# A state-space layer and a mixture of experts on one core: every engine's order, the stage lags and the PSUM banks laid out anew, and the combine weights broadcast over 128 rows instead of 40

## What is computed

```python
x = x + S6(layernorm(x))      # state-space layer, HIDDEN = 256, 16 states, rank 64, 4 taps
x = x + MoE(layernorm(x))     # 8 experts of width 176, top 2, and a shared MLP of width 352

# S6:  u, o = split(x @ W_in.T);  u = silu(conv4(u) + conv_b)
#      delta_lo, b, c = split(u @ W_gate.T);  delta = softplus(delta_lo @ W_delta.T + bias)
#      h_t = exp(A * delta_t) * h_(t-1) + (delta_t * u_t) * b_t      for 256 x 16 states
#      y_t = sum_s h_t * c_t + D * u;   out = (y * sigmoid(o) * o) @ W_out.T
# MoE: scores = softmax(x @ gate_w.T); top-2 weights, normalised, times 2.5 -> combine
#      sum_e combine[e] * (silu(x @ w_gate[e]) * (x @ w_up[e])) @ w_down[e]  + shared MLP
```

## Time and profile before

| | before |
|---|---|
| time, three runs | 1216.91, 1220.03, 1220.68 us; median 1220.03 |
| profiled execution | span 1213.8 us from the first to the last instruction; no time of its own is given beside the span |
| busy over the span | PE 1121.7 us (92%), DVE 1069.3 (88%), POOL 1068.8 (88%), ACT 1003.7 (83%), PEld 918.1 (76%) |
| TensorE clock granted | 0.972 of 2.4 GHz on average |
| DMA engines | 37.0% of their time |

### The profile page before, as it was taken

How to read it: one execution, slowest core, us unless ns; L and a number is a source line. 1 busy time by engine, 2 the same in 40 slices (tenths; PEclk the granted TensorE clock), 3 DMA queues, 4 the chain that set the end, 5 groups by cost and what they waited for, 6 DMA issues and landing times. The chain is left out here.

```text
span 1213.8 us, 25690 instructions
## 1 busy us (share of the span) xinstructions
PE 1121.7 (92%) x9075; PEld 918.1 (76%) x9075; DVE 1069.3 (88%) x1702; ACT 1003.7 (83%) x2115; POOL 1068.8 (88%) x502
## 2 busy tenths in 40 slices
PE   5667999999999999999999999999999999998887
PEld 4445887787878778788887877778777778876676
DVE  5568999999998999999999999999999999998854
ACT  5878888988887898888889888888888888887642
POOL 3899999999998999999999999999999999998820
PEclk8768999999999999999999999999999999998899
DMA  7433444343334434324443433344343334433000
GB/s 195 121 96 81 111 110 110 85 115 85 83 104 108 106 89 115 87 79 107 112 111 80 115 93 78 103 111 111 80 115 102 80 92 110 107 94 91 5 6 9
DMA packets 71481, 115.05 MB, mean 95 GB/s; under 512 B 8173, under 2 KB 30394, under 8 KB 71354
## 3 DMA queue, kind: packets, MB, share of 16 engines
q1 hardware_dynamic: 71354, 113.42, 37.0%
HBM read 41.04 MB, written 5.24 MB: 38 GB/s over the span
## 5 line engine op out<-in xcount | busy, mean ns | idle before, releaser
L423 POOL TENSOR_TENSOR inject<-rep,bc 128x1024 f32<-128x1024 f32 x256 | 605.7, 2392 | 26.3 <-DMA rep<-dd 26.3
L433 POOL TENSOR_TENSOR read<-state,bc 128x1024 f32<-128x1024 f32 x192 | 453.4, 2384 | 11.7 <-DVE state L702 10.2
L702 DVE TENSOR_TENSOR_SCAN state<-decay_ps,inject 128x1024 f32<-128x1024 f32 x192 | 431.6, 2276 | 20.1 <-ACT decay_ps L526 19.3
L526 ACT ACTIVATE decay_ps<-rep,neg_a 128x255 f32<-128x255 f32 x1024 | 425.4, 461 | 8.2 <-DVE state L702 3.4
L1004 PE MATMUL acc_ps<-ffn_down,features 128*128 128x128 f32 (+1 forms) x1792 | 244.8, 281 | 0.5 <-DVE features L731 0.5
L1004 PEld LDWEIGHTS acc_ps<-ffn_down,features 128*128 128x128 f32 (+1 forms) x1792 | 220.3, 192 | 23.2 <-issue 6.6
L970 PE MATMUL work_ps<-xn2T_part,ffn_gate 128*128 128x256 f32 x1344 | 218.4, 299 | 5.8 <-ACT g_silu L513 3.0
L513 ACT ACTIVATE g_silu<-work_ps 128x512 f32<-128x512 f32 x224 | 134.6, 601 | 104.5 <-PE work_ps L970 93.3
L970 PEld LDWEIGHTS work_ps<-xn2T_part,ffn_gate 128*128 128x128 f32 x1344 | 179.4, 192 | 51.3 <-ACT g_silu L513 21.8
L979 PE MATMUL work_ps<-xn2T_part,ffn_up 128*128 128x256 f32 x1344 | 192.5, 283 | 0.0
L723 DVE TENSOR_TENSOR features<-g_silu,work_ps 128x512 f32<-128x512 f32 x224 | 150.0, 681 | 46.0 <-PE work_ps L979 45.4
(11 more groups left out here) (134 smaller groups left out, 1244.5 us busy)
## 6 DMA issues: line engine op xcount, KB each, us to landing
rep<-dd SPq DMA_DIRECT2D x256, 256.0 KB, 4.7
bc<-bc_rows SPq DMA_DIRECT2D x64, 512.0 KB, 4.8
x_in<-in_L_attn_x_dram SPq DMA_DIRECT2D x32, 128.0 KB, 2.1
out_dram<-result SPq DMA_DIRECT2D x32, 128.0 KB, 1.8
bc_rows<-g_sb SPq DMA_DIRECT2D x32, 32.0 KB
state<-in_L_ffn_w_gate_dram SPq DMA_DIRECT2D x1, 704.0 KB, 4.5
inject<-in_L_ffn_w_up_dram SPq DMA_DIRECT2D x1, 704.0 KB, 6.0
ffn_down<-in_L_ffn_w_down_dram SPq DMA_DIRECT2D x1, 704.0 KB, 7.2
```

The costliest lines, as they stand in the source:

```text
L423: pool.tensor_tensor(inject[:, at % RI], du_all, b_all, ALU.mult).then_inc(inject_done, 1)
L433: pool.tensor_tensor(read[:, at % RR], state[:, at % RS], c_all, ALU.mult).then_inc(read_done, 1)
L526: last = act.activation(decay_ps[:, at % 2, j, 1:T], rep[(HALVES * n + half) % RP][:, j, 0, 1:T], ACT.Exp, scale=neg_a[:, col:col + 1])
L702: dve.tensor_tensor_scan(to, decays, inject[:, at % RI].rearrange("p j t -> p (j t)"), 0.0, ALU.mult, ALU.add).then_inc(state_done, 1)
```

## The change

2. The banks change, and so do the explicit waits that guard them:

```diff
-GATE_BANK = [0, 2, 1, 0, 0, 0, 0]
-UP_BANK = [1, 0, 2, 1, 1, 2, 1]
+GATE_BANK = [2, 0, 0, 1, 0, 1, 2]
+UP_BANK = [1, 2, 0, 1, 0, 0, 2]
-COMB_BANK = [0, 1, 0, 1, 0, 1]
+COMB_BANK = [1, 1, 0, 2, 0, 2]
-        combT_ps = banks[1][0:LOW + EXPERTS, 0:T]
+        combT_ps = banks[2][:, 0:T]
-        xnT_ps = banks[2][:, 0:T]        # xn2T_ps and logit_ps likewise go from 2 to 1,
+        xnT_ps = banks[1][:, 0:T]        # marked_ps, inv_ps and comb_ps from 1 to 2
```

3. The combine weights are padded with zeros to 128 rows:

```diff
-        csel = sb("csel", [LOW + EXPERTS, ROUTED], F32R)
+        csel = sb("csel", [P, ROUTED], F32R)
-        comb_parts = sb("comb_parts", [P, TILES, LOW + EXPERTS], F32R)
-        combT = sb("combT", [LOW + EXPERTS, T], F32R)
+        comb_parts = sb("comb_parts", [P, TILES, P], F32R)
+        combT = sb("combT", [P, T], F32R)
```

4. Two of the new order's explicit waits, on PE and on ACT:

```diff
+                if on(2):
+                    pe.wait_ge(u_done, k + 3)
+                if on(-2):
+                    gates(k - 2, 6)
...
+                if on(-2):
+                    act.wait_ge(h_done, PAIRS * (k - 2) + 4)
...
+                if later(1):
+                    softplus(k + 1)
+                    copy_delta(k + 1)
```

More of the change, by code:

```diff
@@ new lines, in copy_z, with softplus, copy_delta @@
+            def copy_z(n):
+                act.wait_ge(delta_done, n)
+                act.wait_ge(z_mm, n + 1)
+                act.copy(z_sb[:], z_ps).then_inc(z_copied, 1)
+            def softplus(n):
+                act.wait_ge(z_copied, n)
+                act.activation(delta_ps, z_sb[:], ACT.Softplus).then_inc(delta_done, 1)
+            def copy_delta(n):
+                act.wait_ge(delta_done, n + 1)
+                for half in range(HALVES):
+                    act.wait_ge(rep_in[half], 16 * JB * n)
+                act.copy(dd[:, :, 0, :], delta_ps).then_inc(dd_done, 1)
@@ L646, in body @@
+                if later(2):
+                    copy_g(k + 2)
                 if on(0):
@@ L671, in body @@
-                if on(1) and k >= 0:
-                    decays(k + 1, 0)
-                    decays(k + 1, 1)
-            step(body, -3)
-            steps(body, -2)
+                if later(2):
+                    copy_z(k + 2)
+                if later(1):
+                    decays(k + 1, 0)
+            log_vars(-4)
+            rstds(-4)
+            act.preload_act_table_set("silu_and_others")
+            norm1(0)
+            xn_high(0)
+            xn_low(0)
+            copy_weights()
@@ new lines, in body @@
+                if on(-2) and not on(1):
+                    dve.wait_ge(h_done, PAIRS * (k - 2) + 2)
+                if on(-2):
+                    route(k - 2)
+                    gated_up(k - 2, 2)
+                    comb_low(k - 2)
+                if on(-3):
+                    add_result(k - 3)
+                if on(0):
+                    scan(k, 2)
+                if on(-1):
+                    add_x1(k - 1)
+                    stats_x1(k - 1)
+                if later(3):
+                    moments_x(k + 3)
@@ new lines, in project_g, with project_z @@
+            def project_g(n):
+                if n == 0:
+                    pe.wait_ge(act_weights, ACT_WEIGHTS)
+                pe.wait_ge(u_done, n + 1)
+                for half in range(HALVES):
+                    last = pe.matmul(g_ps, wg[:, half, :], u[n % RU][:, half, :], start=(half == 0),
+                                     stop=(half == HALVES - 1))
+                last.then_inc(g_mm, 1)
+            def project_z(n):
+                pe.wait_ge(g_done, n + 1)
+                for half in range(HALVES):
+                    last = pe.matmul(z_ps[:, half, :], wdelta[:, half, :], g_sb[:], start=True, stop=True)
+                last.then_inc(z_mm, 1)
@@ new lines, in skip_term, with sum_states @@
+            def skip_term(n, half):
+                pe.matmul(y_ps, skip[:, half, :], u[n % RU][:, half, :], start=True, stop=False, skip_group_check=True)
+            def sum_states(n, q):
+                half, g = divmod(q, SG)
+                if q in OWN:
+                    pe.wait_ge(read_own_done, own(n, q) + 1)
+                    products = read_own
+                else:
+                    pe.wait_ge(read_done, others(n, q) + 1)
+                    products = read[:, others(n, q) % RR]
+                for j in range(JB):
+                    last = pe.matmul(y_ps[j * CB:(j + 1) * CB, :], sum_sel[:], products[:, j, :],
+                                     start=False, stop=(g == SG - 1), skip_group_check=True)
+                last.then_inc(sum_done, 1)
@@ new lines, in down @@
+            def down(n, chunk, fresh=False):
+                r = rows(chunk)
+                if chunk in (0, 2):
+                    pe.wait_ge(h_done, PAIRS * n + chunk // 2 + 1)
+                elif chunk == NSH or chunk % 2 == 0:
+                    pe.wait_ge(hc_done, COMBS * n + (chunk - NSH + 1) // 2 + 1)
+                for j in range(TILES):
+                    last = pe.matmul(down_ps[:, j * DIM:(j + 1) * DIM], features[0:r, chunk, j * P:(j + 1) * P],
+                                     ffn_down[0:r, chunk, :], start=fresh and j == 0, stop=(chunk == CHUNKS - 1),
+                                     skip_group_check=True)
+                last.then_inc(down_mm, 1)
@@ L1032, in body @@
[L1032 to L1036 removed]
+                    gate_rows(k + 1)
+                if on(-1):
+                    pe.wait_ge(y_taken, HALVES * (k - 1) + 2)
+                if on(-3):
+                    down(k - 3, 10)
@@ L1194, in body @@
[L1194 to L1204 removed]
+                    down(k - 2, 4)
```

1298 lines of the change are left out of this document (644 added, 654 removed).

## The result

| | before | after |
|---|---|---|
| time, median of the runs beside each other | 1218.47 us (1215.77 to 1220.68) | 1170.2 us (1168.76 to 1170.26) |
| span of the profiled execution | 1213.8 | 1168.5 |

The ratio is 0.9598, 95% interval 0.9572 to 0.9623. The forecast was 1200.4 us; the gain is more than twice what it said, and the time lies under the range.

A forecast was written before the change was run, and what follows sets the result against it. A loop of waits through POOL, PE and ACT was taken to bound the kernel at 35.0 us; 30 periods x (35.02 - 34.3) = 21.6 saved, 2 lost at the end, span 1194.2, plus 6.2: 1200.4 us, range 1180 to 1232.

The forecast's parts named there:

- ACT's work: ACT's busy time a step: 30.58 us before plus 2.57 for two table loads and 0.2 for gaps, 33.4.
- ends: Before the first and after the last x1: start unchanged, tail 2 us longer from two table loads.
- The loop of before: Sum 6, gates(0), silus, softplus, delta copy, rep spreads, I0, R5, R6: 35.0 us, the old period; 32.0 after the change.
- Wait (a), silu 6: ACT at silu 6 waits 0.45 us for gates(6), which wait for `u`, with only silu 5 between.
- Wait (b), copy_g: ACT at copy_g waits 0.35 to 0.4 us for project_g: PE needs 6.05 us, ACT 5.75.
- (c), xn2_low: PE's rest product done at t + 9.15, ACT there at t + 9.2 (t: end of `u`): no wait, no slack.
- 128 rows: PE's 11 spreads a step, padded from 40 rows, each save 0.06 us, 0.65 in all; without padding period 34.9.
- DVE, POOL, banks, DMA: DVE's pass 33.7 us, POOL's 33.1 plus about 1 of waits, moved b/c spreads hidden, new guards 0.
- the wait for rstd: POOL's wait for ACT's rstd, 66.1 us in all before, would be gone, that for rep kept.
- the third: Rival in which ACT runs without waits: period 33.5 us, 43 us faster, 1177 us; chance 0.12.

The follow-up runs named there:

- x1_before_sum6: Kernel before with PE's sum 6 moved behind ups(2) of the next step, beside sum 7; 1225.04 us, ratio 1.0044.
- y1_after_rows40: Kernel after with the combine weights back at 40 rows in place of 128; 1206.88 us, ratio 0.9889 to the kernel before.
- y4: Kernel after with an eighth table load a step, ahead of copy_z; 1222.89 us, ratio 1.0033 to the kernel before.
- v2b: Kernel after with norm 1 whole between silus 5 and 6 and downs 3 and 4 behind xn2's rest product; 1177.74 us.
- v2c: Kernel after with norm 1 in halves, one between silus 5 and 6, and downs 3 and 4 behind xn2's rest product; 1178.27 us.
- v2a: Kernel after with only downs 3 and 4 moved behind xn2's rest product on PE; 1175.74 us.

## Why the prediction was wrong

The direction was right, and so was the kind of sum for the new period, ACT's work and two waits of it; its terms were off. What failed are two of them: ACT's work, put at 33.4 us and measured at 33.05, and the wait at copy_g, put at 0.35 to 0.4 and measured at 0.10. The reading of the old period was in part wrong as well. Span saved: 19.6 us by the forecast, 45.3 measured. The 25.7 us of difference are

- **the period**, 34.3 against 33.77, and 31 of them in place of 30: 31 x 1.25 - 30 x 0.72 = 17.2;
- **irregular steps**: 5.3. The prediction named 35.11 as the mean and 35.02 as the regular period, and took only the second;
- **ends**: 2 us lost by the forecast, 1.3 gained: 3.3. The two extra loads of the last pass cost nothing that shows.

Step by step:

1. *The loop of before* through sum 6 holds the longer steps only, and x1_before_sum6 cut it and gained nothing. That its times add up to 35.0 proved nothing, since 19.8 us of them, from sum 6 to the copy, were never taken apart, and a round always adds up. And 594.2 for sum 6 one step earlier is not what the trace has: it starts at 593.91, behind a wait of 0.36 us, so the step that was read is one of 35.29 us.
2. *ACT's work*, 33.4 with gaps: measured 33.77 - 0.62 - 0.10 = 33.05. The loads are as forecast (1.28 each, the next instruction 0.01 later). What was missed: neighbours on ACT overlap by 0.1 us when no wait stands between them; the pair of silus takes 1.09 us, not 1.2. Silus 0 to 3 and the gate silu stood apart before, so the busy time of before, 30.58, was too high a start for the sum (32.87 measured against 30.58 + 2.57).
3. *Wait (a), silu 6*: forecast 0.45, measured 0.62. Gates(6) don't wait for `u`; they come directly behind ups(4), which waited for silu 4, and start 0.14 us after `u` is done, not 0.05. G4 releases silu 6 at the same time and was not in the sum.
4. *Wait (b), copy_g*: forecast 0.35 to 0.4, measured 0.10. The handoff is there, and loop 2 hangs on it. Its PE side was right (6.05; here from the end of `u` at 598.80 to that of project_g at 604.79, 5.99, and 0.05 to copy_g), but ACT would come at 5.94, not 5.75, mainly since silu 6 is later. Two numbers of six us, each summed from some ten rows, were subtracted, and 0.4 us of wait were built on an error of 0.3.
5. *(c), xn2_low*: "No wait, but no slack" is exact, and it is loop 1. The prediction left it out of the sum, rightly, but didn't see that it ties the period from a second side.
6. Sum of 2 to 5: 33.05 + 0.62 + 0.10 = 33.77 against 33.4 + 0.45 + 0.4 + 0.05 = 34.3.
7. *128 rows*: forecast 34.9 without them, measured 34.90, and the wait at copy_g, forecast at 0.9 to 1.05, is 0.95. Both are luck. The forecast took 0.6 us a step from padding on a base of 34.3, and it is 1.13 on 33.77; it gave three visits in (b) 0.5 to 0.65, and they cost 0.94 (from ups(4) to the end of project_g 7.60 in place of 6.66), which made up for a wait put 0.3 too high. That a spread of 128 rows goes at 0.118 us is wrong too: in a visit of two they are 0.20 us apart. The expectation of y1_after_rows40 (1186 to 1192 us) missed.
   The Trainium skill ("TensorE: Matmul & The Clock Gate", "Why this matters for your kernels") has a single matmul over 32 rows take the same time as one over 128. By the 0.11 to 0.12 us inside the visit of four the trace agrees for 40 rows, and "the rows speak against it" was a misreading. What the padding saves is the change of row count, 36.7 us here.
8. *DVE, POOL, banks, DMA*: no wait of theirs binds alone, as forecast, but G4 of DVE is level with gates(6). That ACT becomes the fullest engine is wrong (32.87 us against POOL's 33.02); the wait for rstd went from 66.1 us in 34 to the 20.4 us in 4 of the start.
9. *Rivals.* Of the four, the third (ACT runs without waits, 33.5 us, 1177) is nearest, and it had a chance of 0.12. Errors of 0.4 us a step are 12 us of the kernel; the own range of 1188 to 1214 was too narrow for a sum of that many pitches, and "as small as my errors" was the reason to give the rival more.

The table loads cost what the earlier trace rows shows, 1.28 us, and 1.39 with nothing to cover them (y4). The Trainium skill ("ScalarE: Activation LUTs", "What ACT_TABLE_LOAD costs") gives 2.66 us a switch; seven such switches would be 18.6 us, an estimate from that page, and with the 23.9 us of ACT's other busy time that doesn't fit into 33.77. The trace shows 0.02 us ahead of a load and 0.01 behind it.

What the layout as a whole brings is not split into parts: taken out singly, sum 6, the padding and decays 1 cost 0.9, 1.1 and 3.8 us a step, 5.8 in all for a change that gains 1.25, and put in singly they gain nothing or lose. Of the 3.8 about 1.1 are the clock, by the estimate above. v2b and v2c take 2 to 3 us more than v2a at the same period; 1.2 and 1.8 us of it are there at the first x1 (84.1 and 84.7 us against 82.9), and the rest was not traced. Nor were the changes of the banks, the orders of DVE and SP and the b/c spreads tried one by one.

## What to carry to other kernels

When every engine is near full, look for all loops that have no slack, not only the first one found: in the kernel after two were tied, so each single edit was worth nothing and the pair something. The sum of a round proves nothing, it always gives the period; what proves is each handoff without slack, and an edit of one loop that moves the time. A hold of 0.1 us, such as that of copy_g, isn't listed as a wait and can still be the one that counts. A wait of a few tenths got as the difference of two long sums is not a forecast; give the case without it equal weight. And look for a stretch of one engine that is waited for by another (here PE's 9.57 us): a cost in it, such as a change of row count between a few small matmuls, counts in full, while the same cost elsewhere is free.
